# Graph row passes: one tile in 64 fetched row by row from SP and ACT, and a ring of 64 tiles

## The reference

```python
out = d_inv[:, None] * jax.ops.segment_sum(edge_feat[he], src, num_segments=num_nodes)
```

## Time and profile before

| | us |
|---|---|
| median of 3 runs (7760.16 to 7767.0) | 7762.1 |
| the profiled execution's own time | 7762.21 |
| its span, first to last instruction | 7760.5 |
| the four row passes, first gather to last, together | 4807.0 |
| POOL busy in these four windows | 3166.8 |

### The profile page before, as it was taken

The page is one execution under the profiler, slowest core; times in us unless marked ns, Lnnn a source line. Parts: engine busy times, 40 slices in busy tenths (PEclk is TensorE's granted clock), DMA queues, the critical chain, the costliest instruction groups (busy, mean ns, idle before and its releaser), DMA issues. The chain is left out here.

```text
span 7760.5 us, 78987 instructions
## 1 busy us (share of the span) xinstructions
PE 4504.2 (58%) x19204; PEld 3550.5 (46%) x19204; DVE 2722.0 (35%) x7375; ACT 978.8 (13%) x2865; POOL 4410.7 (57%) x4603
## 2 busy tenths in 40 slices
PE   4565554555555555555444444599962656666579
PEld 3444443434444333434333333499841444444368
DVE  3111111222222111111244444422364666666544
ACT  0000000000000000000000000143330000000223
POOL 4666664666666666666666666311135666665345
PEclk8777776777777777776777777799985777777689
DMA  5777775333333333333344444206024444444345
GB/s 146 100 103 101 101 99 96 100 101 99 103 100 102 96 103 103 101 105 104 110 122 123 125 123 125 86 10 198 3 87 122 119 118 120 119 116 112 123 83 88
DMA packets 473127, 814.31 MB, mean 105 GB/s; under 512 B 108347, under 2 KB 331444, under 8 KB 472668
## 3 DMA queue, kind: packets, MB, share of 16 engines
q0 software_dynamic: 222080, 576.78, 33.0%
q1 hardware_dynamic: 249676, 226.09, 9.5%
q10 hardware_dynamic: 1208, 9.86, 0.3%
HBM read 649.02 MB, written 163.60 MB: 105 GB/s over the span
## 5 line engine op out<-in xcount | busy, mean ns | idle before, releaser
L365 POOL DMA_INDIRECT s_rows<-table,ids x2496 | 2382.0, 954 | 1313.7 <-issue 720.0
L628 PE MATMUL s_part<-s_rows,s_onehot 128*128 128x257 f32 x6656 | 2096.3, 463 | 936.9 <-issue 479.6
L628 PEld LDWEIGHTS s_part<-s_rows,s_onehot 128*128 128x128 f32 x6656 | 1532.5, 237 | 1361.1 <-issue 1039.1
L1473 POOL DMA_INDIRECT at_rows<-h_t,ids x832 | 812.0, 976 | 508.2 <-issue 246.7
L467 DVE TENSOR_SCALAR s_inv<-s_raw 128x1 f32<-128x1 f32 x416 | 62.7, 151 | 2869.1 <-ACT s_raw L412 2221.4
L365 POOL DMA_INDIRECT s_rows<-xn_d,ids x832 | 788.5, 948 | 472.2 <-issue 241.9
L601 PE MATMUL s_psY<-w,s_xT 128*128 128x256 f32 x832 | 301.5, 498 | 649.5 <-ACT s_y L394 500.4
L1869 PE MATMUL at_part<-at_rows,at_onehot 128*128 128x264 f32 x1664 | 602.1, 492 | 8.4 <-issue 8.4
L516 DVE TENSOR_TENSOR s_onehot<-s_fixed,rel 128x1024 f32<-128x1024 f32 x416 | 508.6, 1223 | 161.8 <-issue 108.8
L601 PEld LDWEIGHTS s_psY<-w,s_xT 128*128 128x128 f32 x832 | 198.5, 250 | 733.7 <-ACT s_xT L388 336.5
L412 ACT ACTIVATE s_raw<-s_part 128x257 f32<-128x257 f32 x416 | 160.5, 386 | 2464.4 <-DMA acc<-in_x 1066.3
(11 more groups left out here) (363 smaller groups left out, 5633.5 us busy)
## 6 DMA issues: line engine op xcount, KB each, us to landing
s_rows<-table,ids POOLq DMA_INDIRECT x2496
xs_d<-blank SPq DMA_DIRECT2D x38, 1032.0 KB, 12.2
table<-s_y SPq DMA_DIRECT2D x208, 128.0 KB
ex_x<-xs_d SPq DMA_DIRECT2D x60, 258.0 KB
s_rows<-xn_d,ids POOLq DMA_INDIRECT x832
table<-s_x SPq DMA_DIRECT2D x104, 128.0 KB
s_at_node<-in_x SPq DMA_DIRECT2D x104, 128.0 KB
s_at_node<-xn_d SPq DMA_DIRECT2D x104, 128.0 KB
```

The costliest lines, as they stand in the source:

```text
L365: pool.indirect_dma_start(rows[:, t % RT, 0:D], None, table[0:NP_, :], bass.IndirectOffsetOnAxis(cst["ids"][:, t:t + 1], 0)).then_inc(rows ...
L628: ins = pe.matmul(part[u][:, 0:D + 1], onehot[:, u, t % JT, :], rows[:, t, 0:D + 1], start=False, stop=(t == JT * u + JT - 1))
L1473: pool.indirect_dma_start(rows[:, t % AHEAD, :], None, table, bass.IndirectOffsetOnAxis(cst["ids"][:, t:t + 1], 0)).then_inc(rows_in[t % A ...
```

## The change

`RT` goes from 32 to 64 slots, and with it a round from 4 to 8 groups and a pass from 26 to 13 rounds. Of the 64 tiles of a round POOL gathers 63. The rows of the last one are fetched singly, by 128 direct DMAs of one row each: 80 by SP, in five chunks of 16 that stand behind SP's stores of five groups in a row, and 48 by ACT, in six chunks of 8 that stand behind its copies. Each chunk first loads its node numbers into registers (`values_load`), with the check of their bounds left out. A round's rows can be issued once PE has summed the last tile of the round before. PE waits for all 128 before the matmul of tile 63. In s2 the fill that goes to `runs` is made as one sixteenth and stored 16 times. SP and ACT now choose between the two programs (`narrow_or_wide`) as DVE and PE did; with these inputs the first one runs.

```diff
-    RT = 2 * TIT
+    RT = 4 * TIT
...
-            fill = m.sb(f"{name}_fill", [P, NT * H8])
+            fill = m.sb(f"{name}_fill", [P, NT // 2])
...
+        row_in = [m.sem(f"{name}_row_in{q}") for q in range(2)]
+        BY_SP, SP_ROWS, ACT_ROWS = 80, 16, 8
+        SP_LAG = 3 if makes else 1
+
+        def load_rows(eng, eng_type, q, i, at, n):
+
+            src = nc.values_load_multi_w_load_instructions(cst["row_ids"][0:1, bass.ds(P * i + at, n)],
+                                                           engines=[eng_type], min_val=0, max_val=NP_ - 1,
+                                                           skip_runtime_bounds_check_because="node numbers")[1]
+            for k in range(n):
+                eng.dma_start(rows[at + k:at + k + 1, RT - 1, 0:D], table[bass.ds(src[k], 1), :]
+                              ).then_inc(row_in[q], 16)
+
+        def sp_rows(sp, i, c):
+            if SP_ROWS * c < BY_SP:
+                if c == 0 and not (isinstance(i, int) and i == 0):
+                    sp.wait_ge(summed, RT * i + RT)
+                    sp.sem_inc(issue, 1)
+                load_rows(sp, mybir.EngineType.SP, 0, i, SP_ROWS * c, SP_ROWS)
+
+        def act_rows(act, i, c):
+            at = BY_SP + ACT_ROWS * c
+            if at < P:
+                if c == 0 and not (isinstance(i, int) and i == 0):
+                    act.wait_ge(summed, RT * i + RT)
+                    act.sem_inc(issue, 1)
+                load_rows(act, mybir.EngineType.Activation, 1, i, at, min(ACT_ROWS, P - at))
...
                             sp.dma_start(at_node[b][:, c, :], own[c][bass.ds(first[u + 2], P), :]
                                          ).then_inc(node_in[b], 16)
-
-            with sp.Fori(0, ROUNDS - 1) as i:
-                round_of(i, False)
-            round_of(ROUNDS - 1, True)
-            sp.wait_ge(stored, per_store * NJ + STORES)
+                    ahead = (u + SP_LAG) // RG
+                    if not alone and not (last and ahead):
+                        sp_rows(sp, i + ahead, (u + SP_LAG) % RG)
...
+                if t % RT == RT - 1:
+                    continue
                 pool.indirect_dma_start(rows[:, t % RT, 0:D], None, table[0:NP_, :],
...
-                act.dma_start(cst["runs"].rearrange("(p t) h -> p (t h)", p=P), fill[:]).then_inc(fill_stored, 16)
+                for q in range(2 * H8):
+                    act.dma_start(cst["runs"].rearrange("(p t) h -> p (t h)", p=P)[:, q * NT // 2:(q + 1) * NT // 2], fill[:]
+                                  ).then_inc(fill_stored, 16)
...
                 for u in range(RG):
...
+                    ahead = (u + 1) // RG
+                    if not alone and not (ending and ahead):
+                        act_rows(act, i + ahead, (u + 1) % RG)
...
+            def rows_loaded(i):
+                for q, n in enumerate((BY_SP, P - BY_SP)):
+                    pe.wait_ge(row_in[q], 16 * n * i + 16 * n)
...
                             if t % G4 == 0:
-                                pe.wait_ge(rows_in[t // G4], 16 * G4 * i + 16 * G4)
+                                by_pool = G4 - 1 if t + G4 == RT else G4
+                                pe.wait_ge(rows_in[t // G4], 16 * by_pool * i + 16 * by_pool)
                             if t == JT * u:
                                 pe.wait_ge(onehot_ready, 2 * g + 2)
+                            if t == RT - 1:
+                                rows_loaded(i)
```

More of the change, by code:

```diff
@@ L332, in _, with round_of @@
                         sp.dma_start(at_node[b][:, c, :], own[c][bass.ds(first[b], P), :]).then_inc(node_in[b], 16)
-            def round_of(i, last):
+            def round_of(i, last, alone):
                 first = windows(mybir.EngineType.SP, RG * i, RG if last else RG + firsts_of)
@@ L352, in round_of, with program, sp_rows_alone @@
                                          ).then_inc(node_in[b], 16)
-            with sp.Fori(0, ROUNDS - 1) as i:
-                round_of(i, False)
-            round_of(ROUNDS - 1, True)
-            sp.wait_ge(stored, per_store * NJ + STORES)
+                    ahead = (u + SP_LAG) // RG
+                    if not alone and not (last and ahead):
+                        sp_rows(sp, i + ahead, (u + SP_LAG) % RG)
+            def program(joint):
+                alone = joint == 1
+                if alone:
+                    with sp.Fori(0, ROUNDS) as i:
+                        sp.wait_ge(summed, RT * i + RT)
+                        for c in range(RG):
+                            sp_rows_alone(i, c)
+                else:
+                    for c in range(SP_LAG):
+                        sp_rows(sp, 0, c)
+                with sp.Fori(0, ROUNDS - 1) as i:
+                    round_of(i, False, alone)
+                round_of(ROUNDS - 1, True, alone)
+                sp.wait_ge(stored, per_store * NJ + STORES)
+            def sp_rows_alone(i, c):
+                if SP_ROWS * c < BY_SP:
+                    load_rows(sp, mybir.EngineType.SP, 0, i, SP_ROWS * c, SP_ROWS)
+            narrow_or_wide(cst, sp, program)
         @block.gpsimd
@@ L375, in _ @@
                 act.dma_start(by_block[:], degrees[0:NP_, :].rearrange("(b p) o -> b (p o)", p=P)).then_inc(deg_in, 16)
-                act.activation(fill[:], cst["ones"][:, 0:1].to_broadcast([P, NT * H8]), ACT.Copy, scale=-BIG
+                act.activation(fill[:], cst["ones"][:, 0:1].to_broadcast([P, NT // 2]), ACT.Copy, scale=-BIG
                                ).then_inc(filled, 1)
                 act.wait_ge(filled, 1)
-                act.dma_start(cst["runs"].rearrange("(p t) h -> p (t h)", p=P), fill[:]).then_inc(fill_stored, 16)
+                for q in range(2 * H8):
+                    act.dma_start(cst["runs"].rearrange("(p t) h -> p (t h)", p=P)[:, q * NT // 2:(q + 1) * NT // 2], fill[:]
+                                  ).then_inc(fill_stored, 16)
             def copy_turned(k, b, at):
@@ L394, in copy_made, with round_of @@
                 act.activation(y[b][:], psY[:, 0:D], ACT.Copy).then_inc(made_out, 1)
-            def round_of(i, opening):
+            def round_of(i, opening, alone, ending=False):
                 first = None
                 if kind == "last":
-                    first = windows(mybir.EngineType.Activation, 0, 2) if opening else \
+                    first = windows(mybir.EngineType.Activation, 0, RG - 2) if opening else \
                         windows(mybir.EngineType.Activation, RG * i - 2, RG)
@@ L411, in round_of @@
                     act.sem_inc(issue, 1)
-                    act.activation(raw[u][:, 0:D + 1], part[u][:, 0:D + 1], ACT.Copy).then_inc(raw_ready, 1)
+                    act.activation(raw[u % 4][:, 0:D + 1], part[u % 4][:, 0:D + 1], ACT.Copy).then_inc(raw_ready, 1)
                     if kind == "last":
@@ L415, in round_of, with program, finish_rounds @@
                         act.activation(std[:], var[:], ACT.Sqrt).then_inc(std_ready, 1)
[L417 to L425, removed]
+                    ahead = (u + 1) // RG
+                    if not alone and not (ending and ahead):
+                        act_rows(act, i + ahead, (u + 1) % RG)
+            def program(joint):
+                alone = joint == 1
+                if alone:
+                    with act.Fori(0, ROUNDS) as i:
+                        act.wait_ge(summed, RT * i + RT)
+                        for c in range(RG):
+                            act_rows(act, i, c)
+                else:
+                    act_rows(act, 0, 0)
+                round_of(0, True, alone)
+                with act.Fori(1, ROUNDS - 1) as i:
+                    round_of(i, False, alone)
+                round_of(ROUNDS - 1, False, alone, True)
+                finish_rounds()
+            def finish_rounds():
+                first = windows(mybir.EngineType.Activation, NJ - 2, 2) if kind == "last" else None
+                for g in range(NJ, NJ + 3):
+                    if turns and g < NJ + 2:
+                        copy_turned(g - 2, g % 2, first and first[g - NJ])
+                    if makes:
+                        copy_made(g - 3, (g + 1) % 2)
+            narrow_or_wide(cst, act, program)
             if kind == "mid":
-                act.wait_ge(fill_stored, 16)
+                act.wait_ge(fill_stored, 32 * H8)
         @block.vector
```

25 lines of the change are left out of this document (15 added, 10 removed).

## The result

The changed kernel takes 8793.2 us (median of 4 runs, 8782.1 to 8805.7), the kernel before beside it 7764.6 us (4 runs, 7760.2 to 7769.2): a ratio of 1.1325 with a 95% interval of 1.1306 to 1.1345. The forecast was 8340 us in a range of 7500 to 9000 us. The profiled execution has a span of 8780.3 us, 1019.8 us more than before.

A forecast was written before the change was run, and what follows sets the result against it. POOL's gathers were taken as the bound, with SP's slowed row issuing lengthening each round: 52 rounds x 11.1 us = +577 us, the 65 us for gathers included, on 7762 us gives 8340 us; range 7500 to 9000 us.

The forecast's parts named there:

- The mechanism: Round of 64 tiles: late SP stops PE before tile 63, POOL fills the ring and stops, SP turns quick; 11.1 us more.
- W: SP's work in a round if everything is quick (row DMAs, number take-outs, register loads, old work): 60 us, or 72.
- the 0.6 that I named as a sign: Sign of being right: SP issues almost without a break, with row pitches of both 0.6 and 2 us and more.
- 24.6 + 10.7: SP's work during a round's gathers: 24.6 us in quick time, plus 10.7 us worth done in 54.2 slow us.
- 103.5 us: Forecast length of a round of 64 tiles: 54.2 us slow plus 49.3 us quick, 11.1 us more than before.
- The 65 us for the gathers: POOL's gathers in the four passes: 52 removed at a pitch of 1.25 us save 65 us if POOL stays the bound.
- The ring: Ring of 64 slots: can only save POOL's pauses, at most 645 us; counted at nothing in the likeliest case.
- ACT: ACT's 48 row DMAs a round: 39 us of issuing, no slow case seen in its register loads; counted at nothing.
- Packets: 6,656 rows of 1 KB replace as many of POOL's; counted at nothing, 799 us a pass if split in 16.
- The fill and the choice of program: 15 more stores on ACT at the head of s2, 5 us; loads and branches under 2 us a pass; counted as nothing.
- theory A: Experiments' theory: SP's instructions slowed beside POOL's gathers cause the loss; changed kernel 6840 to 6960 us where steps are quick.

## Why the prediction was right, and where it was off

**The mechanism held.** SP is late, PE stops before tile 63, POOL fills the ring and stops, and SP is quick in POOL's pause: each is in the timelines of the round shown above. The run without waits for the rows shows that SP's lateness makes the loss also where nothing waits for the rows, and the run without gathers shows that SP is quick without them. The passes were forecast at 1345 us each, and are 1363 to 1459. POOL's pauses are over 20 us a round, as foreseen: 108.4 - 78.8 = 29.6 us.

**The size of W was off, and its slowing the other way.** I took the take-out of a number from ACT's 0.152 us and the DMA at 0.44 us, 0.59 us a row. SP's instructions for the row DMAs of the changed kernel, ns least, median and most:

```profile
L329 SPq FUSED_REGOPS  x4160: 1/37/1408, 54.9 to 5988.8; - x199
L329 SPq MOVE s_rows<-table x3120: 2/29/1411, 1604.8 to 5988.9; - x195
L329 SPq DMA_DIRECT2D s_rows<-table x3120: 1/228/1407, 1604.8 to 5989.0; - x195
```

Three instructions, and the quick pitch is 0.41 us, not the 0.6 that I named as a sign. The take-out is 37 ns. On line 322, where it is 152 ns, the bounds are checked, and here they aren't; that this is the reason wasn't tested. So 80 rows are 33 us, not 47. With five register loads at 1.2 us (median of SP's on the chip without slow steps) and 5 us for the stores and their registers, W is some 44 us, not 60. Against this I had held SP to be quick for 24.6 us of a round beside POOL's gathers as well, because I read 4 in 10 quick issues as four tenths of the time. From the starts of the rows (the time of a kind of stretch, divided by the rows issued in it): while POOL keeps its pitch it is 1.29 us a row, a speed of 0.41 / 1.29 = 0.32; in POOL's pauses over 1.5 us it is 0.55 us, 0.75. In 78.8 us of gathers SP gets 25 us of its work done, where I had counted 24.6 + 10.7 = 35.3. The remaining 19 us take 25 us of pause, so a round is 104 us by this account, and 108.4 were measured. The two errors took each other up: 103.5 us was forecast, and that it came so near is in part luck. The profiled execution went 443 us beyond the forecast (1020 - 577); the missing 4.9 us a round are 254 us of them (831 - 577).

**The ends of the passes were left out.** Some 195 us more are 149 us between the passes and 46 us before the attention stage. The forecast multiplied a round by 52 and forgot that the last round has to be worked off once POOL is done. The ring alone explains 58 of the 149 us, the run with the ring alone showing 88, 43 and 24 us. SP's rows make it more: where only SP's rows are issued, s1's end takes 118 us on the chip with slow steps and 116 us on the one without.

**Gathers and ring.** The 65 us for the gathers measured 75. The ring counted at nothing and cost 1.0% by itself, with no pause saved, as the attention stage's pauses had suggested.

**ACT.** I counted nothing; it is 2.1%, 164 us. It was taken that ACT's register loads show no slow case. ACT's row DMAs do: their mean pitch is 1.00 us for a quick one of 0.38. 25 loads and 98 take-outs in one pass had been too few to tell.

**Packets, fill, choice.** The page's row of the direct DMAs' larger queue (packets, MB, share of 16 engines):

```profile
q1 hardware_dynamic: 257998, 230.37, 8.7%
```

That is 8322 packets more than the 249,676 of before for 4160 rows of SP, two each, so a row wasn't split in 16; the queue's share is 8.7% of the longer span where it was 9.5%. Packets were no cost. The fill and the choice of program were not measured by themselves; they are within the ratio of 0.9995 for the run without rows.

**Register loads, and issuing from several engines.** By the Trainium skill (Runtime: NRT & Kernel Launch, section Instruction fetch mechanics) a register load is about 200 ns for a register. No run here shows that for SP, whose loads here read a tile in SBUF, where the page speaks of loads from HBM: its 260 loads of 16 numbers have a median of 1133 ns in the changed kernel, 71 ns a number, and of 1200 ns on the chip without slow steps. ACT's 312 loads of 8 numbers have a median of 721 ns, 90 ns a number, so the 0.23 us read from its loads of four was no price for a longer load either. The Trainium skill (DMA: Bandwidth & Descriptors, section Issuing engines are not separate DMA queues) says that starting DMAs on several engines saves only sequencer time, "which is usually small relative to the DMA itself". On the chip without slow steps the runs nearly agree: SP's rows cost 46 us there, 0.7%. On the others the sequencer's time was the whole price.

**What stays open.** What the steps of 0.70 us are, and why one chip had none on the one occasion that it was used. That they come with POOL's gathers is shown by the run without them and by the stages of the kernel before; whether POOL's issuing or the traffic of the gathers does it wasn't separated; that the gathers are not enough is shown by the chip that gathers at the same pitch without slow steps. Whether the changed kernel itself is slower there wasn't measured: the run of it fell on a chip with slow steps, so theory A's figure for the other kind (0.995 to 1.012) stands untested.

## What to carry to other kernels

Before work is moved to an engine that "only issues", add up that engine's waits over the stretch: SP's 714 us of waiting looked like room for 80 more DMAs a round, but on chips with slow steps its instructions cost 0.36 to 0.39 us each on the mean of a pass, and 240 more of them a round filled it. Count instructions, not bytes or DMAs, and check what else stands in the same queue: here it was the stores that free the next buffers. Where a profile shows quick and slow steps of one instruction, measure on more than one chip before a price is put on either.

## What the runs showed of the hardware that was not expected

- One program takes 7761, 7762 and 7837 us on three occasions and 6876 us on another chip. Of the 879 us between the two profiled executions (7762.21 and 6883.62), 619 are in the row passes (4807 and 4188) and 197 in the attention stage's gathers (1268 and 1071). There SP's issues have no slow steps and POOL has no pauses behind PE's sums.
- Register instructions of 0.6 us and more are 13% of all in the row passes of the kernel before, 5% in the attention's gathers, 0.4% between the two and none behind them; on the other chip there is none in the whole trace.
- A semaphore increment of 17 ns is caught in these steps (up to 1409 ns) as a DMA issue is (up to 1407 ns).
- A direct DMA of one row of 1 KB is issued by SP in 0.41 us and by ACT in 0.38 us, three instructions, when nothing slows them.
